# Decoder layer on one core: the rotary work of the next group of heads moved one step later on VectorE and GpSimd

## Chip, cores and metric

The kernel runs on 1 core of a Trainium2 chip. The metric is the device time of one launch in microseconds (us). Five engines work side by side, each through its own list of instructions in order: PE (TensorE: matmuls and their weight loads), ACT (ScalarE), DVE (VectorE), POOL (GpSimd) and SP (SyncE, which here only issues DMAs). They meet at semaphores alone.

## The reference, cut to what matters

Three stages follow each other: self-attention, a cross-attention with gathered neighbours, and a quantised feed-forward. The change touches only the first.

```python
# x: (4, 1024, 256), 16 heads of 64
q = (x @ wq.T + bq); k = (x @ wk.T + bk); v = (x @ wv.T + bv)      # per head
q, k = rope(q, k)              # x * cos + rotate(x) * sin, pairs of columns
scores = q k^T, causal; attn = softmax(scores / 8)
x = layernorm(x + (attn @ v) @ wo.T + bo)
...
```

## The kernel before

Self-attention is written as one list of instructions for each engine. Four heads make a group (16 groups, index `i`), two heads make a pair (32 pairs, index `n`, with `i, p = divmod(n, 2)`). A pair goes through six steps `m`. In each step PE computes two blocks ("units", `u = 2m, 2m+1`) of scores for pair `n`, multiplies the probabilities of the step before into the values (`weigh`), and then does the step's extra work (`step_uses`, line 86): chunks of scores of pair `n + 1`, from which the row maxima are taken, and one bigger item of `FULL_AT` (line 42).

The extra work of an even pair is the projection of q and k of the next group, in four parts, at steps 0, 2, 3 and 4 (below: part 0 to part 3); that of an odd pair is the output projection of the group before (steps 0 and 1) and the value projection (steps 2 and 4). Each part goes through three engines:

- ACT copies it from PSUM to SBUF (`stage`, line 602, the copy is line 608). There are two buffers `staged`, so `stage` of part `u` first waits until GpSimd has finished part `u - 2` (semaphore `s_rot`, line 607).
- DVE does four scalar_tensor_tensor instructions (`rotate`, line 699; lines 716 and 720), each of 128x512 float32: bias and multiplication with the cosine or sine table.
- GpSimd adds up the terms (`turn`, line 929; lines 935 and 936).

The row maxima take this way: PE makes a chunk (nine for a pair; in an even pair chunks 0 to 2 at step 1, 3 and 4 at step 2, 5 and 6 at step 3, 7 and 8 at step 4), ACT copies it negated in bfloat16 (line 570, three buffers), DVE masks it (line 767, chunks 0 to 4) and takes the minimum (lines 773 and 778). After chunk 8 DVE makes the negated maxima (`negate`, line 785), PE spreads them into a row in PSUM (`max_row`, line 440, matmul line 448), ACT copies the row (line 561), and PE adds it to the scores of the next pair (`shift`, line 477). `max_row` is the last thing PE does in a pair: until it is through, no score of the next pair is begun.

The probabilities: ACT takes the exponential of each unit (line 626), GpSimd zeroes the corner above the diagonal (`mask_probs`, line 898) and adds the unit to a running sum (`add_probs`, lines 916 and 919). Units 8 and 9 belong to step 4, units 10 and 11 to step 5. DVE also multiplies the output of the pair before by the inverse sums (`normalise`, line 798).

PSUM is handed out as a ring of three slots in PE's order of use (`slot_order`, `wait_slot`, line 244): each use waits until the third use before it has been read. At the end of an even pair the order is unit 8, unit 9, chunk 7, chunk 8, part 3 of the projection, unit 10, unit 11, row. So `max_row` waits for two things: for `negate` (line 442), and for ACT's copy of part 3 (line 257). ACT does that copy after the exponentials of units 8 and 9 and before those of units 10 and 11.

What sets the order around the change is the code itself: DVE's loop is lines 849 to 883, GpSimd's lines 950 to 963.

Of the kernel before, what the change touches and what calls it, by code (L numbers as in the profile page):

```python
# [38 lines left out]
QK_UNITS = 4  # L39
# [35 lines left out]
def full_at(n, m):  # L75

    i, p = divmod(n, 2)
    if not FULL_AT[p][m]:
        return None
    kind, u = FULL_AT[p][m]  # L80
    if kind == "out":
        return (kind, i - 1, u) if i else None
    return (kind, i + 1, u) if i + 1 < GROUPS else None


def step_uses(n, m):

    full = full_at(n, m)
    chunks = [("max", n + 1, c) for c in CHUNKS_AT[n % 2][m]] if n + 1 < PAIRS else []
    if m == 1:  # L90
        sums = [("den", n - 1, 0)] if n else []
        return ([full] if full else []) + chunks[:-1] + sums + chunks[-1:]
    if m == 2 and n % 2:
        return ([full] if full else []) + chunks
    return chunks + ([full] if full else [])
# [28 lines left out]
def attention(nc, dram, y, psum):  # L124

    ctx = ExitStack()
    with ctx:
# [568 lines left out]
        def _(dve):  # L696
            V = nc.vector

            def rotate(i, u):

                m = QK_UNITS * i + u
                hf, qk = divmod(u, 2)
                tok = slice(hf * BANK, (hf + 1) * BANK)
                ev, od = staged[m % 2][:, 0, :], staged[m % 2][:, 1, :]
                be, bo = (bqk[:, i % NG, 2 * qk + eo:2 * qk + eo + 1] for eo in range(2))
                tu = turned[:, :, qk, tok]
                dve.wait_ge(s_stage, m + 1)
                if u == 0 and i == 0:
                    dve.wait_ge(s_bqk, 16)
                if u == 0 and i:  # L710
                    for p in range(2):
                        dve.wait_ge(s_ops[p], 16 * STACK_DMAS * i)
                if i == 0:
                    dve.wait_ge(s_tab[hf], 16)
                for dst, x, b, table in ((tu[:, 0, :], ev, be, cosE), (tu[:, 1, :], od, bo, cosO)):
                    V.scalar_tensor_tensor(out=dst, in0=x, scalar=b, in1=table[:, tok], op0=ALU.add, op1=ALU.mult)\  # L716
                     .then_inc(s_term, 1)
                dve.wait_ge(s_term, TERMS * m + 2)
                for x, b, table in ((ev, be, sinO), (od, bo, sinE)):
                    V.scalar_tensor_tensor(out=x, in0=x, scalar=b, in1=table[:, tok], op0=ALU.add, op1=ALU.mult)\  # L720
                     .then_inc(s_term, 1)
# [127 lines left out]
            for n in range(PAIRS):  # L849
                i, p = divmod(n, 2)  # L850
                new_x = p == 1 and i % NG == 2 and i // NG + 1 < B
                for m in range(STEPS):
                    for kind, k, u in step_uses(n, m):
                        if kind == "max":
                            maximum(k, u)
                        elif kind == "out":
                            residual(k, u)
                    if m == 2 and n:
                        invert(n - 1)
                    if m == LAST_CHUNKS:  # L860
                        if n + 1 < PAIRS:
                            negate(n + 1)
                        if n:
                            normalise(n - 1)
                    if full_at(n, m) and full_at(n, m)[0] == "qk":
                        rotate(i + 1, full_at(n, m)[2])
                    if p == 1 and m == 0 and i + 1 < GROUPS:
                        low_v(i + 1)
                    if p == 1 and m == 1 and i + 2 < GROUPS:
                        for kt in range(KT):  # L870
                            low_qk(i + 2, kt)
                    if p == 1 and m < 2 and i >= NG and i % NG == 1:
                        row_statistics(i // NG - 1, m)
                    if p == 1 and m == 1 and i >= NG and i % NG >= 2:
                        normalise_rows(i // NG - 1, i % NG - 2)
                    if new_x and m == 3:
                        for piece in range(KT):
                            low_x(i // NG + 1, piece)
                    if p == 1 and m >= 4 and i % NG == 0:
                        add_bias(i // NG, m - 4)  # L880
                if new_x:
                    for piece in range(KT, X_PIECES):
                        low_x(i // NG + 1, piece)
# [6 lines left out]
        @block.gpsimd  # L890
        def _(pool):
            G = nc.gpsimd

            def mask_probs(n, u):

                pool.wait_ge(s_exp, NU * n + u + 1)
                block = probs[u % PBUF][:, :, 0:P]
                G.affine_select(block, block, [[0, 2], [1, P]], ALU.is_ge, 0.0, base=0, channel_multiplier=-1)\  # L898
                 .then_inc(s_tri, 1)

            def add_probs(n, u):

                k = NU * n + u
                kt, hf, a, width = span(u)
                if u in DIAGONAL:
                    pool.wait_ge(s_tri, len(DIAGONAL) * n + DIAGONAL.index(u) + 1)
                else:
                    pool.wait_ge(s_exp, k + 1)
                if u == 0 and n == 0:
                    pool.wait_ge(s_split, X_PIECES)  # L910
                if u == 0 and n >= 2:
                    pool.wait_ge(s_den, n - 1)
                dst = acc[n % 2][:, :, a:a + width]
                src = probs[u % PBUF][:, :, 0:width]
                if kt == 0:
                    G.tensor_copy(dst, src).then_inc(s_acc, 1)
                else:
                    pool.wait_ge(s_acc, k)
                    G.tensor_tensor(dst, dst, src, ALU.add).then_inc(s_acc, 1)  # L919

            def deviations(b):
                pool.wait_ge(s_avar, b + 1)
                if b:
                    pool.wait_ge(s_ax1, 2 * b)
                G.tensor_scalar(a_rstd[:, :], a_mv[:, :, 1], EPS, None, ALU.add).then_inc(s_adev, 1)
                pool.wait_ge(s_adev, b + 1)
                G.tensor_tensor(a_rstd[:, :], a_rstd[:, :], a_power[:, :], ALU.pow).then_inc(s_astd, 1)

            def turn(i, u):

                m = QK_UNITS * i + u
                hf, qk = divmod(u, 2)
                tu = turned[:, :, qk, hf * BANK:(hf + 1) * BANK]
                pool.wait_ge(s_term, TERMS * (m + 1))
                G.tensor_tensor(tu[:, 0, :], tu[:, 0, :], staged[m % 2][:, 1, :], ALU.subtract).then_inc(s_rot, 1)
                G.tensor_tensor(tu[:, 1, :], tu[:, 1, :], staged[m % 2][:, 0, :], ALU.add).then_inc(s_rot, 1)

            G.memset(a_power[:, :], -0.5).then_inc(s_set, 1)
            G.memset(ones[:, :], 1.0).then_inc(s_set, 1)
            G.memset(negz[:, :, :, :], 0.0).then_inc(s_set, 1)  # L940
            G.memset(first[:, :], 0.0).then_inc(s_set, 1)
            pool.wait_ge(s_set, 4)
            G.memset(first[0:1, :], 1.0).then_inc(s_set, 1)
            pool.wait_ge(s_set, 5)
            G.memset(first[D:D + 1, :], 1.0).then_inc(s_set, 1)
            pool.wait_ge(s_set, 6)
            G.memset(lows[:, :, :], 1e38).then_inc(s_set, 1)
            for u in range(QK_UNITS):
                turn(0, u)
            for n in range(PAIRS):  # L950
                i, p = divmod(n, 2)
                for m in range(STEPS):
                    for u in (2 * m, 2 * m + 1):
                        if u in DIAGONAL:
                            mask_probs(n, u)
                    if p == 1 and m == 0 and i + 1 < GROUPS:
                        turn(i + 1, QK_UNITS - 1)
                    for u in (2 * m, 2 * m + 1):
                        add_probs(n, u)
                    if p == 0 and m and full_at(n, m - 1) and full_at(n, m - 1)[2] < QK_UNITS - 1:  # L960
                        turn(i + 1, full_at(n, m - 1)[2])
                if i >= NG and i % NG == 1 and p == 1:
                    deviations(i // NG - 1)

# [1479 lines left out]
```

## Time and profile before

| | |
|---|---|
| median of three runs | 2231.85 us (2228.64 to 2235.41) |
| the profiled execution, its own time | 2232.63 us |
| its span, first to last instruction | 2230.7 us |
| busy PE, DVE, POOL, ACT over the span | 84%, 71%, 63%, 59% |
| self-attention | about 57 to 1375 us of the span |
| one group of self-attention (two pairs) | about 82 us |
| PE busy from 400 to 500 us | 94.06 of 100 us |
| PE idle before `max_row` (line 448), 60 to 1270 us | 35.2 us in 15 places |

The timeline views list an engine's instructions in order of time: start, duration (from the first start to the last end of a merged row), engine, line, operation, what is written and read, how many, and in brackets how long the engine was idle before it and what ended that. Two instructions of one engine may overlap in the record by a few hundredths of a microsecond. The duration of a DVE or POOL instruction includes time in which it has begun and is held up. Pairs repeat with small differences; the stretch around 509.55 us, the end of an even pair, is followed closely.

### The profile page before, as it was taken

To read this page: it belongs to the slowest core of one execution; us is meant where nothing else is said; L and a number is where in the kernel's file an instruction comes from. 1 tells how busy PE (TensorE), PEld (TensorE's weight loads), DVE (VectorE), ACT (ScalarE), POOL (GpSimd) and SP (SyncE) were. 2 spreads that over 40 slices of the span, in tenths; PEclk is the share of its full clock that TensorE was granted. 3 is DMA by queue.
4 is the path that set the end of the run, shared out by engine and by line. 5 is a ranking of instruction groups with operands and counts; after the bars stand their busy time and mean duration, and the time that the engine had idled before them with its cause. 6 is when DMAs were issued, how large, how long until landed. Compare 5 with 4: busy or idle time off the path is not lost. (4 is left out here: it accounts for less than half of the span.)

```text
span 2230.7 us, 42278 instructions
## 1 busy us (share of the span) xinstructions
PE 1864.7 (84%) x16907; PEld 1122.3 (50%) x16907; DVE 1593.3 (71%) x2216; ACT 1312.8 (59%) x1718; POOL 1410.0 (63%) x1067
## 2 busy tenths in 40 slices
PE   6899989999989999989999996588787787883675
PEld 3445545555545555545555543366565566663332
DVE  6775776776776776776776762668769768679676
ACT  3565565565565565565565561286856756873466
POOL 2877757777857877757877773344654555545347
PEclk8999999999999999999999998799988898997786
DMA  6122222222222222222222110100000000100002
GB/s 212 42 53 53 49 71 51 51 53 53 49 71 49 53 53 53 48 70 50 53 53 53 39 39 25 54 3 7 2 7 2 2 2 2 43 3 1 2 1 76
DMA packets 57507, 92.33 MB, mean 41 GB/s; under 512 B 25312, under 2 KB 35552, under 8 KB 53344
## 3 DMA queue, kind: packets, MB, share of 16 engines
q1 hardware_dynamic: 48096, 89.36, 16.0%
q8 instruction: 134, 2.20, 0.4%
q10 hardware_dynamic: 9216, 0.27, 0.2%
q14 instruction: 61, 0.50, 0.1%
HBM read 51.33 MB, written 4.46 MB: 25 GB/s over the span
## 5 line engine op out<-in xcount | busy, mean ns | idle before, releaser
L919 POOL TENSOR_TENSOR acc<-acc,probs 128x1024 f32<-128x1024 f32 (+3 forms) x320 | 592.2, 1851 | 149.9 <-ACT probs L626 121.1
L626 ACT ACTIVATE probs<-psum 128x1024 f32<-128x1024 f32 (+3 forms) x384 | 290.9, 812 | 139.7 <-PE psum L477 139.7
L570 ACT ACTIVATE chunks<-psum 128x1024 bf16<-128x1024 f32 x288 | 278.1, 1027 | 83.4 <-PE psum L436 60.4
L1478 ACT ACTIVATE onehot<-psum 128x1024 bf16<-128x1024 f32 x320 | 323.0, 1038 | 1.3 <-PE psum L1288 1.3
L469 PE MATMUL psum<-operands 64*128 64x512 f32 (+3 forms) x1536 | 308.4, 520 | 17.6 <-ACT chunks L570 17.2
L1885 POOL TENSOR_TENSOR vs<-vs,wgt 128x1280 f32<-128x1280 f32 x64 | 156.3, 2443 | 250.8 <-DVE wgt L1729 250.8
L1306 PE MATMUL psum<-pieces,onehot 128*128 128x64 bf16 x7680 | 289.4, 199 | 26.8 <-ACT vs L1485 19.5
L1306 PEld LDWEIGHTS psum<-pieces,onehot 128*128 128x128 bf16 x7680 | 261.0, 102 | 89.1 <-issue 45.3
L493 PE MATMUL psum<-probs,vals 128*64 128x512 f32 (+3 forms) x1536 | 292.6, 499 | 11.8 <-POOL probs L898 11.8
L773 DVE TENSOR_REDUCE lows<-chunks 128x2 f32<-128x1024 bf16 (+1 forms) x224 | 265.4, 1215 | 22.5 <-ACT chunks L570 11.4
L716 DVE SCALAR_TENSOR_TENSOR turned<-staged,bqk,rot 128x512 f32<-128x512 f32 x128 | 150.1, 1212 | 114.0 <-ACT staged L608 114.0
L898 POOL TENSOR_SCALAR_AFFINE_SELECT probs<-probs 128x256 f32<-128x256 f32 x256 | 144.5, 582 | 107.8 <-ACT probs L626 107.8
L767 DVE TENSOR_TENSOR chunks<-chunks,later 128x512 bf16<-128x512 bf16 (+1 forms) x160 | 122.8, 768 | 123.3 <-ACT chunks L570 123.3
L469 PEld LDWEIGHTS psum<-operands 64*128 64x128 f32 x1536 | 130.4, 189 | 148.3 <-issue 80.1
L1695 DVE TENSOR_TENSOR prod<-psum,xq 128x320 f32<-128x320 f32 x256 | 124.0, 488 | 109.4 <-PE psum L1306 104.5
L1485 ACT ACTIVATE vs<-psum 128x320 f32<-128x320 f32 x256 | 114.9, 449 | 147.2 <-DVE prod L1695 146.6
L1288 PE MATMUL psum<-i0T,near 32*128 32x512 bf16 x640 | 131.5, 411 | 82.4 <-ACT onehot L1478 76.0
L720 DVE SCALAR_TENSOR_TENSOR staged<-staged,bqk,rot 128x512 f32<-128x512 f32 x128 | 183.9, 1475 | 2.3
L493 PEld LDWEIGHTS psum<-probs,vals 128*64 128x64 f32 x1536 | 93.1, 136 | 159.0 <-issue 143.5
L436 PE MATMUL psum<-operands 64*128 64x512 f32 (+3 forms) x768 | 118.5, 397 | 38.7 <-ACT probs L626 18.7
L420 PE MATMUL psum<-wo,ctxT 128*128 128x256 f32 x512 | 120.5, 389 | 11.4 <-DVE ctxT L798 11.4
L436 PEld LDWEIGHTS psum<-operands 64*128 64x128 f32 x768 | 58.7, 188 | 131.2 <-issue 59.8
(228 smaller groups left out, 3331.2 us busy)
## 6 DMA issues: line engine op xcount, KB each, us to landing
operands<-turned SPq DMA_DIRECT2D x124, 256.0 KB, 4.2
rden<-inverse_rows SPq DMA_DIRECT2D x64, 256.0 KB, 4.0
raw<-in_wqk SPq DMA_DIRECT2D x30, 256.0 KB, 4.5
y<-in_x SPq DMA_DIRECT2D x1, 4096.0 KB, 16.3
wo<-in_wo SPq DMA_DIRECT2D x16, 256.0 KB, 3.2
out<-res SPq DMA_DIRECT2D x16, 256.0 KB, 2.1
raw<-in_wv SPq DMA_DIRECT2D x15, 256.0 KB, 4.4
raw<-in_xT SPq DMA_DIRECT2D x12, 256.0 KB, 4.4
```

Source lines behind the costliest of these rows:

```text
L436: last = nc.tensor.matmul(dst[:, hh, col:col + width], ops[p][rows, 0, qt * P:(qt + 1) * P], ops[p][rows, 1, hf * BANK:hf * BANK + width], ...
L469: nc.tensor.matmul(dst[:, hh, 0:width], ops[n % 2][rows, 1, kt * P:(kt + 1) * P].bitcast(F32), ops[n % 2][rows, 0, a:a + width].bitcast(F3 ...
L493: last = nc.tensor.matmul(obank[rows, hf, a - hf * BANK:BANK], vals[i % 2][:, kt, 2 * p + hh, :], probs[u % PBUF][:, hh, 0:width], start=k ...
L570: nc.scalar.activation(chunks[k % MBUF][:, :, :], slot("max", n, c)[:, :, :], ACT.Copy, scale=-1.0)\
L626: nc.scalar.activation(probs[u % PBUF][:, :, 0:width], slot("s", n, u)[:, :, 0:width], ACT.Exp, scale=1.0 / D ** 0.5).then_inc(s_exp, 1)
L716: V.scalar_tensor_tensor(out=dst, in0=x, scalar=b, in1=table[:, tok], op0=ALU.add, op1=ALU.mult)\
L720: V.scalar_tensor_tensor(out=x, in0=x, scalar=b, in1=table[:, tok], op0=ALU.add, op1=ALU.mult)\
L773: V.tensor_reduce(lows[:, :, place_of[0]:place_of[-1] + 1:step], src[:, :, 0:len(parts) * width].rearrange("p h (k q) -> p h k q", q=width ...
L919: G.tensor_tensor(dst, dst, src, ALU.add).then_inc(s_acc, 1)
L1306: last = nc.tensor.matmul(out, onehot[:, n % 2, k, tok:tok + P], pieces[b % 2][p][:, h, :, :].rearrange("p (s c) d -> p s (c d)", s=2), st ...
L1478: A.activation(onehot[:, n % 2, k, :], bc[m % 2], ACT.Relu).then_inc(s_oh, 1)
L1885: G.tensor_tensor(v, v, w.broadcast_to([P, TT * NK * 2, HD]), ALU.mult).then_inc(s_wm, 1)
```

## The change

In an even pair DVE's rotation of a part now comes one step later. Part 0, projected at step 0, is rotated at step 1 behind chunks 0 to 2; part 1 at step 3 behind chunks 5 and 6; part 2 at step 4 behind chunks 7 and 8, `negate` and `normalise`; part 3 at step 5. GpSimd's `turn` of parts 0, 1 and 2 also comes one step later: at the ends of steps 2, 4 and 5 instead of 1, 3 and 4. `turn` of part 3 stays at step 0 of the odd pair. PE, ACT and SP keep their order word for word, and no instruction is added or removed. The last group has nothing to project, so 15 even pairs are touched.

```diff
@@ DVE, the loop over steps
-                    if full_at(n, m) and full_at(n, m)[0] == "qk":
-                        rotate(i + 1, full_at(n, m)[2])
+                    if p == 0 and m and full_at(n, m - 1):
+                        rotate(i + 1, full_at(n, m - 1)[2])
@@ GpSimd, the loop over steps
-                    if p == 0 and m and full_at(n, m - 1) and full_at(n, m - 1)[2] < QK_UNITS - 1:
-                        turn(i + 1, full_at(n, m - 1)[2])
+                    if p == 0 and m > 1 and full_at(n, m - 2) and full_at(n, m - 2)[2] < QK_UNITS - 1:
+                        turn(i + 1, full_at(n, m - 2)[2])
```

DVE, even pair, from the reciprocal in step 2 to the first residual of the odd pair, before:

```order
L790 RECIPROCAL rcol<-dcol 128x16
L716 SCALAR_TENSOR_TENSOR turned<-staged1,bqk,rot 128x512 x2
L720 SCALAR_TENSOR_TENSOR staged1<-staged1,bqk,rot 128x512 x2
L773 TENSOR_REDUCE lows<-chunks2 128x2
L773 TENSOR_REDUCE lows<-chunks0 128x2
L716 SCALAR_TENSOR_TENSOR turned<-staged0,bqk,rot 128x512 x2
L720 SCALAR_TENSOR_TENSOR staged0<-staged0,bqk,rot 128x512 x2
L773 TENSOR_REDUCE lows<-chunks1 128x2
L773 TENSOR_REDUCE lows<-chunks2 128x2
L785 TENSOR_TENSOR negmax<-lows 128x16
L798 TENSOR_TENSOR ctxT<-osum1,rden 128x1024
L716 SCALAR_TENSOR_TENSOR turned<-staged1,bqk,rot 128x512 x2
```

The same stretch of DVE after:

```order
L790 RECIPROCAL rcol<-dcol 128x16
L773 TENSOR_REDUCE lows<-chunks2 128x2
L773 TENSOR_REDUCE lows<-chunks0 128x2
L716 SCALAR_TENSOR_TENSOR turned<-staged1,bqk,rot 128x512 x2
L720 SCALAR_TENSOR_TENSOR staged1<-staged1,bqk,rot 128x512 x2
L773 TENSOR_REDUCE lows<-chunks1 128x2
L773 TENSOR_REDUCE lows<-chunks2 128x2
L785 TENSOR_TENSOR negmax<-lows 128x16
L798 TENSOR_TENSOR ctxT<-osum1,rden 128x1024
L716 SCALAR_TENSOR_TENSOR turned<-staged0,bqk,rot 128x512 x2
L720 SCALAR_TENSOR_TENSOR staged0<-staged0,bqk,rot 128x512 x2
L716 SCALAR_TENSOR_TENSOR turned<-staged1,bqk,rot 128x512 x2
```

Between the reciprocal and `negate` (L785) stood two rotations; now one stands there, that of part 1, behind chunks 5 and 6, and the rotation of part 2 stands behind `normalise`.

GpSimd, even pair, steps 3 to 5, before (the first row is the sum of unit 7):

```order
L919 TENSOR_TENSOR acc0<-acc0,probs3 128x2x512
L935 TENSOR_TENSOR turned<-turned,staged1 128x512
L936 TENSOR_TENSOR turned<-turned,staged1 128x512
L898 AFFINE_SELECT probs0<-probs0 128x2x128
L898 AFFINE_SELECT probs1<-probs1 128x2x128
L919 TENSOR_TENSOR acc0<-acc0,probs0 128x2x512
L919 TENSOR_TENSOR acc0<-acc0,probs1 128x2x384
L935 TENSOR_TENSOR turned<-turned,staged0 128x512
L936 TENSOR_TENSOR turned<-turned,staged0 128x512
L898 AFFINE_SELECT probs2<-probs2 128x2x128
```

The same stretch of GpSimd after:

```order
L919 TENSOR_TENSOR acc0<-acc0,probs3 128x2x512
L898 AFFINE_SELECT probs0<-probs0 128x2x128
L898 AFFINE_SELECT probs1<-probs1 128x2x128
L919 TENSOR_TENSOR acc0<-acc0,probs0 128x2x512
L919 TENSOR_TENSOR acc0<-acc0,probs1 128x2x384
L935 TENSOR_TENSOR turned<-turned,staged1 128x512
L936 TENSOR_TENSOR turned<-turned,staged1 128x512
L898 AFFINE_SELECT probs2<-probs2 128x2x128
L898 AFFINE_SELECT probs3<-probs3 128x2x128
L919 TENSOR_TENSOR acc0<-acc0,probs2 128x2x256
```

The end of part 1 (`staged1`) stood ahead of the masks and sums of units 8 and 9; it now stands behind them.

## Rows read from the trace of the kernel before

**Rows 1.** The waits of PE, 60 to 1270 us: total, times, longest.

```profile
PE psum L448 <- DVE negmax L785: 35.2, 15, 3.3
```

**Rows 2.** All engines, 504 to 514 us: the rows of PE around `max_row`.

```profile
505.55 1.72 PE L493 MATMUL psum<-probs,vals 128*64 128x512 f32 x8
...
509.55 0.64 PE L448 MATMUL psum<-ident,negmax 128*64 128x128 bf16 x16 [2.28 <-DVE negmax L785]
...
512.66 0.65 PE L493 MATMUL psum<-probs,vals 128*64 128x256 f32 x4 [0.39 <-POOL probs L898]
...
513.47 0.44 PE L493 MATMUL psum<-probs,vals 128*64 128x128 f32 x4 [0.16 <-POOL probs L898]
...
513.84 0.48 PE L420 MATMUL psum<-wo,ctxT 128*128 128x256 f32 x1
```

**Rows 3.** Timeline of DVE, 498 to 512 us.

```profile
502.95 3.56 DVE L720 SCALAR_TENSOR_TENSOR staged<-staged,bqk,rot 128x512 f32<-128x512 f32 x2
506.44 2.33 DVE L773 TENSOR_REDUCE lows<-chunks 128x2 f32<-128x1024 bf16 x2
508.81 0.69 DVE L785 TENSOR_TENSOR negmax<-lows 128x16 bf16<-128x16 f32 x1
509.36 1.21 DVE L798 TENSOR_TENSOR ctxT<-osum,rden 128x1024 f32<-128x1024 f32 x1
```

**Rows 4.** Timeline of ACT, 494 to 513 us.

```profile
498.99 1.73 ACT L626 ACTIVATE probs<-psum 128x1024 f32<-128x1024 f32 x2 [0.41 <-PE psum L477]
501.45 1.94 ACT L570 ACTIVATE chunks<-psum 128x1024 bf16<-128x1024 f32 x2 [0.74 <-PE psum L436]
504.64 1.03 ACT L608 ACTIVATE staged<-psum 128x1024 f32<-128x1024 f32 x1 [1.25 <-PE psum L383]
505.60 0.87 ACT L626 ACTIVATE probs<-psum 128x512 f32<-128x512 f32 x2
```

**Rows 5.** Timeline of POOL, 491 to 514 us.

```profile
503.16 5.03 POOL L919 TENSOR_TENSOR acc<-acc,probs 128x1024 f32<-128x1024 f32 x2
508.15 1.25 POOL L935 TENSOR_TENSOR turned<-turned,staged 128x512 f32<-128x512 f32 x1
509.37 2.33 POOL L936 TENSOR_TENSOR turned<-turned,staged 128x512 f32<-128x512 f32 x1
```

**Rows 6.** Rotary instructions, 100 to 1250 us: min/median/max ns, first and last start.

```profile
L716 DVE SCALAR_TENSOR_TENSOR turned<-staged,bqk,rot x108: 659/887/2884, 139.6 to 1243.7; 128x512 f32<-128x512 f32 x108
L720 DVE SCALAR_TENSOR_TENSOR staged<-staged,bqk,rot x109: 739/1747/2869, 98.6 to 1249.3; 128x512 f32<-128x512 f32 x109
L936 POOL TENSOR_TENSOR turned<-turned,staged x54: 1260/1280/2332, 103.0 to 1233.8; 128x512 f32<-128x512 f32 x54
```

**Rows 7.** Timeline of POOL in an odd pair: mask and sums of units 8, 9.

```profile
461.92 0.41 POOL L898 TENSOR_SCALAR_AFFINE_SELECT probs<-probs 128x256 f32<-128x256 f32 x1 [0.29 <-ACT probs L626]
462.29 2.37 POOL L919 TENSOR_TENSOR acc<-acc,probs 128x1024 f32<-128x1024 f32 x1
...
464.80 1.85 POOL L919 TENSOR_TENSOR acc<-acc,probs 128x768 f32<-128x768 f32 x1
```

**Rows 8.** Timelines of ACT and POOL at step 2 of the even pair.

```profile
483.27 1.02 ACT L570 ACTIVATE chunks<-psum 128x1024 bf16<-128x1024 f32 x1 [1.26 <-DVE lows L778]
...
486.45 2.39 POOL L919 TENSOR_TENSOR acc<-acc,probs 128x1024 f32<-128x1024 f32 x1
```

**Rows 9.** Timeline of PE at another end of an even pair.

```profile
426.80 1.06 PE L448 MATMUL psum<-ident,negmax 128*64 128x128 bf16 x16 [2.27 <-DVE negmax L785]
...
431.87 0.92 PE L420 MATMUL psum<-wo,ctxT 128*128 128x256 f32 x3
```

**Rows 10.** Stretches of 2 us from `max_row` on: length, busy of each engine, PE clock.

```profile
95.38:97.38 2.00, 2.00 (x20) 1.32 (x22) 2.00 (x2) 1.02 (x1) 2.00 (x3) 0.59 0.00 0
...
426.80:428.80 2.00, 2.00 (x18) 1.32 (x20) 2.00 (x2) 0.90 (x1) 2.00 (x1) 0.51 0.02 4
509.55:511.55 2.00, 2.00 (x24) 1.26 (x26) 2.00 (x2) 1.02 (x1) 2.00 (x1) 1.00 0.00 0
```

## The prediction

> **What bounds the kernel now.** I read the busy shares first: PE is busy for 94 of the 100 us from 400 to 500 in self-attention, so a change there pays only where it shortens a place at which PE itself stands still. The second view is PE's waits. The largest is that of `max_row` for DVE's negated maxima: 35.2 us in 15 places, one at the end of each even pair from the first to the 15th [rows 1]. That is 1.6% of the time, and it is what this change can reach. The third view is the timeline around one of them. PE has finished its last weighting at 507.27 (505.55 + 1.72) and starts `max_row` at 509.55, after 2.28 us of nothing [rows 2]. On DVE the second half of part 2's rotation runs until 506.51, then the maxima of chunks 7 and 8 until 508.77, then `negate` until 509.50 [rows 3]. Those chunks lay copied since 503.39 (501.45 + 1.94) [rows 4]. So DVE's rotation of part 2 is in the way, and the change moves it behind.
>
> **Two waits, not one.** `max_row` also waits, through the ring of PSUM slots, for ACT's copy of part 3, and that copy waits for GpSimd's end of part 1, since both use the same staging buffer. Before, the copy ran at 504.64 to 505.67, as soon as PE had projected the part [rows 4], long before `max_row`, so this second wait does not show. The change moves GpSimd's end of part 1 from ahead of the sums of units 8 and 9 to behind them. The question is when it is through then.
>
> **Walk of the changed order, in the stretch that ends at 509.55.** PE, ACT and SP keep their order and their times up to the first new wait. Four durations carry it: a rotation instruction takes 0.66 or 0.74 us undisturbed (minima, against maxima of 2.88 and 2.87), `turn`'s second 1.26 us undisturbed against 2.33 at worst [rows 6], the sums of units 8 and 9 2.37 and 1.85 us and a mask 0.41 beside DVE work that reads one tensor [rows 7]. The large values arise where DVE and GpSimd both want to run an instruction on two SBUF tensors: the one that comes second does not progress until the first is through. The clearest row: GpSimd's second `turn` instruction, 509.37 with 2.33 us, lies over `normalise`, 509.36 to 510.57, and ends 1.13 us behind it [rows 3, 5].
>
> 1. Chunk 2 is copied at 484.29 (483.27 + 1.02) [rows 8]. Mask and minimum take about 1.7 us, so rotation 0 starts at 486.0. One of its instructions runs before GpSimd's sum of unit 5 (2.39 us) [rows 8], three behind it: 486.9, 489.3, then 3 x 0.7: done at 491.4.
> 2. GpSimd's end of part 0 (2 x 1.26) alternates with the masks of chunks 3 and 4 on DVE (estimated at 0.3 each): done at 494.7. ACT needs it for part 2's copy at 497: 2.4 us to spare, price nothing. Chunks 3 and 4 are read by 495.9 (the masks and two minima of 1.2 to 1.3 us each; the nearest row is 2.33 for two minima [rows 3]). Their buffers are wanted again at 494.8 (chunk 3, read at 493.2) and at 501.45: free.
> 3. Sums 6 and 7 on GpSimd, 2 x 2.37 from 494.7: 499.4. Minima of chunks 5 and 6 on DVE: 498.3. Rotation 1 waits for sum 7, then alternates with the masks of units 8 and 9, whose exponentials end by 500.72 (498.99 + 1.73) [rows 4]: 499.4 + 2 x 0.66 + 2 x 0.74 gives 502.2; the masks fall in between.
> 4. Minima of chunks 7 and 8 from 502.5, held by the copy that ends at 503.39: done 504.8. Sums 8 and 9 on GpSimd from 502.2: 504.6, then 506.5. `negate` needs two tensors and waits for that: 506.5, which is 0.8 before PE wants it. **The wait that the change aims at is gone**: -2.28 us at this place, if nothing else were late.
> 5. GpSimd's end of part 1: behind `normalise` (1.1, as between 509.50 and 510.57 [rows 3]) and 2 x 1.26: 506.5 + 1.1 + 2.5 = 510.1. ACT's copy of part 3: 510.15 + 1.03 [rows 4] = 511.2. `max_row` starts at 511.25 instead of 509.55: **+1.7 us**, and PE stands still for 4.0 us instead of 2.28. ACT's exponentials of units 10 and 11 stand behind that copy; they end at 512.1 (0.87 [rows 4]) and PE's next scores need them only from about 511.9 and 512.8 on.
> 6. What comes back at once: before, PE waited another 0.39 and 0.16 us for the masks of units 10 and 11 [rows 2]. Now these come ahead of GpSimd's end of part 2, right behind the exponentials, so I count the 0.55 as gone: from `max_row` to the output projection 4.29 us becomes 3.74. That end moves from 513.84 to 514.99: **+1.15 us**.
>
> Rotations 2 and 3 then run on DVE from about 508 to 517; the residual that follows them waits for an output projection that ends near 518.5, so they cost nothing. GpSimd's end of part 3 slips by about 2 us; its operands are wanted some 10 us later. If either cover fails it would show as a new wait in the odd pair; I put no price on it. Nothing in the odd pair gives the loss back: PE is busy throughout.
>
> **The clock.** After the idle time PE sometimes runs at the lower level. At 426.80 the granted clock is 0.51 (1.2 GHz), and 5.07 us pass until the output projection; at 509.55 it is 1.00 (2.4 GHz) and 4.29 pass [rows 2, 9, 10]. Of the 15 places 5 show this, 10 don't, the one with 3.3 us of idle time among the 5 [rows 1, 10]. An idle time of 4.0 us has no row. Bounds: the same 5, or all 15. I take 10, half-way, since the longest idle time fell and two thirds of the 2.3 us ones didn't. The Trainium skill says on this (TensorE: Matmul & The Clock Gate, Part 1) that "the default state is throttled, and activity releases the throttle". By that rule the longer standstill would put more places at the low level, nearer to all 15, which is the upper bound below.
>
> **The sum.** A place at full clock before and after costs 1.15; one that was low before and stays low costs 1.7 (5.07 on both sides); one that becomes low costs 511.25 + 5.07 - 513.84 = 2.5. With 5 of each: 5 x 1.15 + 5 x 1.7 + 5 x 2.5 = 26.7 us. On the profiled execution's own 2232.63 that is 2259.4; the median shown lies 0.8 below that execution, so I say **2259**, 1.2% slower.
>
> **Rivals.**
>
> *Faster, about 2216.* DVE and GpSimd meet less often than I let them. Without any holding-up the masks are through at 501.2, the sums at 505.5, the end of part 1 at 508.0, ACT's copy at 509.1: `max_row` starts 0.45 early and the output projection is reached 1.0 early: 15 x 1.0 = 15 us less; with a shorter idle time up to 5 x 0.8 more: 2213 to 2218. For it: the masks of chunks and the negation are short. Against it: an L720 takes 1.75 us in the median against 0.74 alone [rows 6], so meeting is the rule here. The point from which it decides: the end of part 1 before about 508.5. The Trainium skill (SBUF — State Buffer, the reading of its port diagram) calls the pair of ports shared by the two engines an exclusive lock that is held for the whole instruction. By that rule the two-tensor work of both engines adds up from 486 on, which is the walk above, 2259; if the two only slowed each other in part, it would be this rival. The 2.33 us row agrees with the rule.
>
> *No change, 2226 to 2238.* One holding-up less than in the walk, for example if the end of part 1 gets ahead of `normalise` and rotation 1 is out of GpSimd's way earlier: the end at 508.9 to 509.2, `max_row` at about 510.1: +0.55 - 0.55 = 0 at the output projection, and a few us for the clock either way.
>
> *Slower still, 2266 to 2275.* All 15 places at the low level: 5 x 1.7 + 10 x 2.5 = 33.5, that is 2266. If a rotation instruction also gets between the two of `turn`, 0.6 more at 15 places: 2275.
>
> *The change does not do what it says.* The negation could still be last, if rotation 1 ran beyond 505; then the maxima of chunks 7 and 8 end after 507.3. That needs 3 us more than in step 3 and would come together with a still later end of part 1, so its time is that of the case above.
>
> **How the numbers follow.** Forecast (2239 to 2265) 0.60; slower still 0.12; no change 0.14; faster 0.14. A measurement of this kernel can tell about 0.3%, 6.7 us, from no change. So faster 0.14, same 0.14, slower 0.72. For the range I leave out the faster rival and the outermost few per cent above 2272: 2228 to 2272, which holds the lower half of "no change" and the bounds of the clock.
>
> **What would show it.** Right: PE's wait at `max_row` is put down to ACT's copy of part 3 (L608), not to L785, 15 times at about 4 us; that copy is ended by GpSimd's L936; L785 ends before PE's last weighting; the waits for L898 behind it shrink; more stretches with a clock near 0.5. Wrong in step 5: the copy starts by 508. Wrong in the cover: a new wait in the odd pairs, for the operands or the residual.

## The result and the profile after

The changed kernel takes 2278.17 us (median of four runs, 2273.97 to 2280.74) against 2233.27 us for the kernel before (four runs): a ratio of 1.0209, 95% interval 1.0186 to 1.0233. It is slower by 45 us. The forecast was 2259 us, slower by 27, with a range up to 2272. So the sign and the wait were right, and the time lies outside the range.

The waits of PE in self-attention, 60 to 1320 us of the changed kernel (total, times, longest; it answers [rows 1]):

```profile
PE psum L448 <- ACT staged L608: 60.3, 15, 4.1
PE psum L436 <- ACT probs L626: 17.0, 17, 4.2
```

`max_row` still waits at 15 places, now for ACT's copy of part 3, and for 60.3 us instead of 35.2: 3.04 us at the first place and 4.07 to 4.11 at the other 14. The timeline of PE around one of the places (it answers [rows 2]):

```profile
520.28 1.72 PE L493 MATMUL psum<-probs,vals 128*64 128x512 f32 x8
526.08 1.06 PE L448 MATMUL psum<-ident,negmax 128*64 128x128 bf16 x16 [4.07 <-ACT staged L608]
527.07 3.36 PE L469 MATMUL psum<-operands 64*128 64x512 f32 x8
530.22 0.96 PE L477 MATMUL psum<-bias,first_rows 64*128 64x512 bf16 x4
531.11 0.94 PE L493 MATMUL psum<-probs,vals 128*64 128x256 f32 x8
531.98 0.70 PE L420 MATMUL psum<-wo,ctxT 128*128 128x256 f32 x2
```

PE is through at 522.00 and idle for 4.07 us; then 5.90 us pass until the output projection, where it was 4.29. The other three engines over the same stretch, DVE first (it answers [rows 3]):

```profile
512.29 2.38 DVE L716 SCALAR_TENSOR_TENSOR turned<-staged,bqk,rot 128x512 f32<-128x512 f32 x2
514.71 1.56 DVE L720 SCALAR_TENSOR_TENSOR staged<-staged,bqk,rot 128x512 f32<-128x512 f32 x2
517.31 2.35 DVE L773 TENSOR_REDUCE lows<-chunks 128x2 f32<-128x1024 bf16 x2 [1.04 <-ACT chunks L570]
519.69 1.26 DVE L785 TENSOR_TENSOR negmax<-lows 128x16 bf16<-128x16 f32 x1
520.82 1.21 DVE L798 TENSOR_TENSOR ctxT<-osum,rden 128x1024 f32<-128x1024 f32 x1
521.95 3.41 DVE L716 SCALAR_TENSOR_TENSOR turned<-staged,bqk,rot 128x512 f32<-128x512 f32 x2
```

POOL (it answers [rows 5]):

```profile
516.51 4.36 POOL L919 TENSOR_TENSOR acc<-acc,probs 128x1024 f32<-128x1024 f32 x2
520.82 2.33 POOL L935 TENSOR_TENSOR turned<-turned,staged 128x512 f32<-128x512 f32 x1
523.11 1.70 POOL L936 TENSOR_TENSOR turned<-turned,staged 128x512 f32<-128x512 f32 x1
```

ACT (it answers [rows 4]):

```profile
524.91 1.02 ACT L608 ACTIVATE staged<-psum 128x1024 f32<-128x1024 f32 x1 [6.79 <-POOL turned L936]
525.83 0.87 ACT L626 ACTIVATE probs<-psum 128x512 f32<-128x512 f32 x2
```

The negation is ready at 520.95, 1.05 us before PE wants it: the wait that the change aims at is gone. GpSimd begins the end of part 1 only behind both sums, at 520.82; `normalise` and one rotation instruction get in between, it is done at 524.81, ACT's copy at 525.93, `max_row` starts at 526.08.

The clock, in stretches of 2 us from `max_row` on, and for the 5.90 us (it answers [rows 10]; the third column from the right is PE's granted clock):

```profile
97.00:99.00 2.00, 2.00 (x20) 1.14 (x22) 2.00 (x4) 1.64 (x3) 1.58 (x3) 0.70 0.00 0
...
526.08:528.08 2.00, 2.00 (x18) 1.32 (x20) 2.00 (x4) 1.52 (x3) 1.59 (x3) 0.50 0.00 0
...
526.08:531.98 5.90, 5.90 (x36) 2.87 (x36) 5.12 (x6) 2.73 (x5) 5.34 (x5) 0.56 0.00 0
```

The first place reads 0.70 and each of the other 14 reads 0.50, the level of 1.2 GHz. Before, 5 of 15 were below 1.00.

**Where the 45 us are.** The spans differ by 44.7 us (2275.4 against 2230.7). PE's waits at `max_row` grew by 60.3 - 35.2 = 25.1 us. From `max_row` to the output projection the timeline gives 5.9 to 6.2 us at each of 14 places (the first place has no such projection), 5.98 in the mean, where it gave 4.29 ten times and 5.1 four times, 4.52 in the mean: 14 x 1.46 = 20.4 us. Together 45.5. Two smaller differences nearly cancel and are not in this sum. Up to `max_row` of the 16th even pair, which begins at 1379.75 and began at 1330.98, the kernel is 48.8 us longer, about 3 more than these two, and they lie in the first group. From there to the end it takes 895.7 us instead of 899.7; the code there is the same, and the 12 traces of this case give 889 to 909 us for it, so a few microseconds between two single traces say nothing.

### The profile page after: what moved, and what is told of

Its sections match the earlier page's. It is cut to its first block and busy times, and to the rows that moved or that the text cites. A ratio compares the mean times of both kernels' runs of the same rounds, so it can differ in the third digit from the quotient of the medians.

```text
span 2275.4 us, 42278 instructions
## 1 busy us (share of the span) xinstructions
PE 1886.7 (83%) x16907; PEld 1129.5 (50%) x16907; DVE 1526.6 (67%) x2216; ACT 1310.6 (58%) x1718; POOL 1386.5 (61%) x1067
## 5 line engine op out<-in xcount | busy, mean ns | idle before, releaser
L919 POOL TENSOR_TENSOR acc<-acc,probs 128x1024 f32<-128x1024 f32 (+3 forms) x320 | 573.5, 1792 | 97.2 <-ACT probs L626 68.7
L626 ACT ACTIVATE probs<-psum 128x1024 f32<-128x1024 f32 (+3 forms) x384 | 290.8, 812 | 157.3 <-PE psum L477 155.0
L469 PE MATMUL psum<-operands 64*128 64x512 f32 (+3 forms) x1536 | 325.5, 544 | 17.6 <-ACT chunks L570 17.2
L773 DVE TENSOR_REDUCE lows<-chunks 128x2 f32<-128x1024 bf16 (+1 forms) x224 | 264.8, 1213 | 37.1 <-ACT chunks L570 26.3
L767 DVE TENSOR_TENSOR chunks<-chunks,later 128x512 bf16<-128x512 bf16 (+1 forms) x160 | 93.8, 586 | 289.7 <-ACT chunks L570 289.7
L898 POOL TENSOR_SCALAR_AFFINE_SELECT probs<-probs 128x256 f32<-128x256 f32 x256 | 132.5, 535 | 152.9 <-ACT probs L626 152.9
L469 PEld LDWEIGHTS psum<-operands 64*128 64x128 f32 x1536 | 135.4, 196 | 154.8 <-issue 87.5
L716 DVE SCALAR_TENSOR_TENSOR turned<-staged,bqk,rot 128x512 f32<-128x512 f32 x128 | 175.6, 1410 | 15.5 <-ACT staged L608 15.5
L608 ACT ACTIVATE staged<-psum 128x1024 f32<-128x1024 f32 x64 | 65.7, 1026 | 185.1 <-POOL turned L936 108.0
L916 POOL COPY acc<-probs 128x1024 f32<-128x1024 f32 x64 | 66.5, 1040 | 149.0 <-ACT probs L626 149.0
L436 PE MATMUL psum<-operands 64*128 64x512 f32 (+3 forms) x768 | 119.0, 399 | 37.5 <-ACT probs L626 17.3
L935 POOL TENSOR_TENSOR turned<-turned,staged 128x512 f32<-128x512 f32 x64 | 105.9, 1655 | 51.7 <-DVE staged L720 51.7
```

The lines of the kernel that those rows point to most:

```text
L469: nc.tensor.matmul(dst[:, hh, 0:width], ops[n % 2][rows, 1, kt * P:(kt + 1) * P].bitcast(F32), ops[n % 2][rows, 0, a:a + width].bitcast(F3 ...
L626: nc.scalar.activation(probs[u % PBUF][:, :, 0:width], slot("s", n, u)[:, :, 0:width], ACT.Exp, scale=1.0 / D ** 0.5).then_inc(s_exp, 1)
L773: V.tensor_reduce(lows[:, :, place_of[0]:place_of[-1] + 1:step], src[:, :, 0:len(parts) * width].rearrange("p h (k q) -> p h k q", q=width ...
```

## The experiments

All times below stand beside runs of the kernel before on the same chip, 2232 to 2233 us in the median. The changed kernel was timed once, beside 2233.27 us, so a difference from it may be off by a microsecond or two. Timelines are those of one profiled execution each, which is not always near the median of its kernel (e6_part2_only: 2196.83 against 2206.56 us).

**One half of the change alone.** First the rotations on VectorE, with GpSimd's order as before.

```diff
# against the kernel before
-                    if full_at(n, m) and full_at(n, m)[0] == "qk":
-                        rotate(i + 1, full_at(n, m)[2])
+                    if p == 0 and m and full_at(n, m - 1):
+                        rotate(i + 1, full_at(n, m - 1)[2])
```

> VectorE's rotations stand as in the changed kernel, GpSimd's ends of parts 0 to 2 stand as in the kernel before (part 1 ahead of the masks and sums of units 8 and 9). Theory (the late end of part 1 on GpSimd is what costs): ScalarE's copy of part 3 is no longer late by much, max_row's wait of 4.1 us for it is gone or under 1 us; what is left is that GpSimd stands waiting for rotations with masks behind it, about +-0.5 us a place, so 2225 to 2245 us. Rival (the later rotations on VectorE are what costs, wherever GpSimd's ends stand): as slow as the changed kernel, 2265 to 2280 us.

Measured: 2326.87 us, ratio 1.0432 (1.0407 to 1.0458). Neither expectation. No wait for L448 is left, as the theory said, but PE's timeline shows another one behind it:

```profile
445.93 0.65 PE L448 MATMUL psum<-ident,negmax 128*64 128x128 bf16 x16
...
455.71 1.55 PE L493 MATMUL psum<-probs,vals 128*64 128x256 f32 x8 [7.06 <-POOL probs L898]
```

and POOL's timeline tells why:

```profile
451.38 1.71 POOL L935 TENSOR_TENSOR turned<-turned,staged 128x512 f32<-128x512 f32 x1 [1.29 <-DVE staged L720]
453.05 1.70 POOL L936 TENSOR_TENSOR turned<-turned,staged 128x512 f32<-128x512 f32 x1
454.71 1.67 POOL L898 TENSOR_SCALAR_AFFINE_SELECT probs<-probs 128x256 f32<-128x256 f32 x2
```

GpSimd stands waiting for rotation 2, then ends part 2, and the masks of units 10 and 11 are queued behind that; PE waits 7 us for them. I had priced this at 0.5 us. So GpSimd's end of part 2 had to be moved with its rotation; the change is right in that.

**The other half**, GpSimd's ends one step later and the rotations as before:

```diff
# against the kernel before
-                    if p == 0 and m and full_at(n, m - 1) and full_at(n, m - 1)[2] < QK_UNITS - 1:
-                        turn(i + 1, full_at(n, m - 1)[2])
+                    if p == 0 and m > 1 and full_at(n, m - 2) and full_at(n, m - 2)[2] < QK_UNITS - 1:
+                        turn(i + 1, full_at(n, m - 2)[2])
```

> GpSimd's ends stand as in the changed kernel, VectorE's rotations as in the kernel before. Theory: the end of part 1 stands behind the sums of units 8 and 9 all the same, so max_row waits for ScalarE's copy of part 3 at 15 places, some 3 to 4 us each, and the clock falls at most of them: 2262 to 2280 us. Rival (VectorE's order is what costs): max_row waits for the negated maxima as before, 2228 to 2240 us.

Measured: 2296.03 us, ratio 1.0293 (1.0266 to 1.032), 16 us above the upper end that I expected. `max_row` waits 5.67 us at each of 15 places, and the profile names DVE's negation, not ACT's copy. DVE's timeline:

```profile
523.06 4.50 DVE L716 SCALAR_TENSOR_TENSOR turned<-staged,bqk,rot 128x512 f32<-128x512 f32 x2
527.60 3.31 DVE L720 SCALAR_TENSOR_TENSOR staged<-staged,bqk,rot 128x512 f32<-128x512 f32 x2
...
533.20 0.92 DVE L785 TENSOR_TENSOR negmax<-lows 128x16 bf16<-128x16 f32 x1
```

and PE's:

```profile
534.18 1.07 PE L448 MATMUL psum<-ident,negmax 128*64 128x128 bf16 x16 [5.67 <-DVE negmax L785]
```

Rotation 2 now runs beside the two sums and the end of part 1 on GpSimd, one instruction of each in turn: its four instructions take 7.85 us, where undisturbed they take 2.8 [rows 6]. ACT's copy of part 3 is late as the theory had it (81.6 us of waits for L936 in 14 places): it ends at 531.48, 2.97 us behind PE's last weighting (528.51), and the negation, done at 534.12, is later still. GpSimd's half alone is therefore enough for a loss, by both ways at once; with both halves together the negation is out of it. The granted clock is 0.50 behind each of the 15 waits of 5.67 us.

**Only the end of part 1 put back ahead of the sums**, everything else as changed:

```diff
# against the changed kernel, GpSimd
                     for u in (2 * m, 2 * m + 1):
                         if u in DIAGONAL:
                             mask_probs(n, u)
...
+                    if p == 0 and m == 4 and full_at(n, 2):
+                        turn(i + 1, 1)
                     for u in (2 * m, 2 * m + 1):
                         add_probs(n, u)
-                    if p == 0 and m > 1 and full_at(n, m - 2) and full_at(n, m - 2)[2] < QK_UNITS - 1:
+                    if p == 0 and m in (2, 5) and full_at(n, m - 2) and full_at(n, m - 2)[2] < QK_UNITS - 1:
                         turn(i + 1, full_at(n, m - 2)[2])
```

> The changed kernel with one instruction pair of GpSimd put elsewhere: the end of part 1 stands ahead of the sums of units 8 and 9, behind their masks. Theory: ScalarE's copy of part 3 comes by about 505 in the frame of the prediction, the negated maxima by 507, and both waits of max_row are gone: 2.28 us less than before at 15 places and the clock stays up, 2192 to 2203 us. Rival (the loss comes from several places and GpSimd being behind everywhere): the time stays above 2240 us.

Measured: 2229.94 us, ratio 0.9991 (0.9977 to 1.0005). Moving this pair of instructions takes 48 us off the changed kernel, which settles what the loss hung on; but the gain of 30 us and more that I expected is not there. PE's timeline:

```profile
507.31 0.62 PE L448 MATMUL psum<-ident,negmax 128*64 128x128 bf16 x16
...
510.69 0.65 PE L493 MATMUL psum<-probs,vals 128*64 128x256 f32 x4 [0.67 <-POOL probs L898]
...
518.42 3.18 PE L493 MATMUL psum<-probs,vals 128*64 128x512 f32 x8 [1.81 <-ACT probs L626]
```

`max_row` starts with no wait. Waits for the masks of units 10 and 11 (0.67 and 0.16 us) are back, and a larger one stands at step 1 of the odd pair, 25.4 us in 14 places. It is put down to L626, the exponentials, but those ended at 511.6; the masks of units 0 and 1 are what came last, as POOL shows:

```profile
514.12 1.71 POOL L935 TENSOR_TENSOR turned<-turned,staged 128x512 f32<-128x512 f32 x1
515.79 1.71 POOL L936 TENSOR_TENSOR turned<-turned,staged 128x512 f32<-128x512 f32 x1
517.46 1.67 POOL L898 TENSOR_SCALAR_AFFINE_SELECT probs<-probs 128x256 f32<-128x256 f32 x2
```

The end of part 2 stands ahead of those masks. At this place PE then runs at the lower level for a while: the eight matmuls take 3.18 us, and over the 3.2 us from 518.4 on the granted clock is 0.52. But only one other of the 14 places is like this; at the other 12, behind the same 1.81 us, the clock over the next 2 us is 1.00 (at 436.75 the eight matmuls take 1.72 us). The gain went to waits: 35.2 us for the negation and 7.1 for masks (L898) before, now 25.4 and 12.3, and 5.5 at step 1 of the first odd pair.

**The standstill filled.** This takes the clock alone. TensorE does 17 more matmuls in the wait; their output is overwritten and nothing depends on it.

```diff
# against the changed kernel, TensorE, ahead of max_row
+                if p == 0 and i + 1 < GROUPS:
+                    pe.wait_ge(s_oc, 2 * n + 1)
+                    for _ in range(17):
+                        nc.tensor.matmul(obank[:, 0, :], ident[:, :], bias[n % 2][:, 0:BANK], start=True, stop=True)
                 if n + 1 < PAIRS:
                     max_row(n + 1)
```

> The changed kernel, and TensorE does 17 further matmuls of 128x512 bfloat16 (about 3.7 us at 2.4 GHz) between its last weighting and max_row at the 15 places, into a half of the output bank that is free then; their result is overwritten and not used. Theory (half of the loss is the clock that falls after the standstill): max_row starts where it did, the granted clock there is 1.00 instead of 0.50, the 5.9 us from max_row to the output projection become 3.7 to 4.3, so 14 x 1.6 to 2.2 = 22 to 31 us less than the changed kernel: 2247 to 2256 us. Rival (the clock does not depend on the standstill, or the slow stretch is slow for another reason): 2275 to 2282 us, or more if the matmuls outlast the wait.

Measured: 2243.49 us, ratio 1.0047 (1.0031 to 1.0064). That is 34.7 us less than the changed kernel, more than expected. PE's timeline (of the fastest of ten executions, 2234.8 us; four added lines make the copy of part 3 L612 and the filling L548):

```profile
512.08 3.84 PE L548 MATMUL psum<-bias,ident 128*128 128x512 bf16 x17
516.25 0.64 PE L448 MATMUL psum<-ident,negmax 128*64 128x128 bf16 x16 [0.33 <-ACT staged L612]
516.82 1.77 PE L469 MATMUL psum<-operands 64*128 64x512 f32 x8
...
519.70 0.70 PE L420 MATMUL psum<-wo,ctxT 128*128 128x256 f32 x2
```

`max_row` waits for the same copy to the same moment, 4.1 us behind the last weighting (512.14), and the granted clock is 1.00 at all 15 places. Now 3.45 us pass until the output projection, at each of 14 places. So 5.98 - 3.45 = 2.53 us a place is the price of the standstill beyond its own length, 14 x 2.53 = 35 us, which is what the medians say (34.7).

**`normalise` out of the way of the end of part 1.**

```diff
# against the changed kernel, VectorE
-                        if n:
+                        if n and (p or i + 1 == GROUPS):
                             normalise(n - 1)
+                    if m == STEPS - 1 and n and p == 0 and i + 1 < GROUPS:
+                        normalise(n - 1)
```

> The changed kernel with normalise of an even pair moved from step 4 to step 5, behind the rotation of part 2. Theory (step 5 of the prediction: GpSimd's end of part 1 is also held up by normalise, 1.1 us): TensorE stands still before max_row for about 3.0 us instead of 4.08; the clock still falls at most of the places, so 15 x 1.1 = 16 us less, 2258 to 2266 us. Rival (something else takes normalise's turn, since a rotation instruction is next in line): the idle time stays at 3.6 to 4.1 us and the time at 2270 to 2280 us.

Measured: 2256.89 us, ratio 1.01 (1.0069 to 1.013). PE's timeline and three stretches of 2 us from `max_row` on (the profiled execution is the fastest of four, 2247.77 us):

```profile
516.87 0.64 PE L448 MATMUL psum<-ident,negmax 128*64 128x128 bf16 x16 [3.03 <-ACT staged L608]
```

```profile
516.87:518.87 2.00, 2.00 (x20) 1.22 (x22) 2.00 (x3) 1.64 (x3) 1.58 (x2) 0.68 0.00 0
600.46:602.46 2.00, 2.00 (x18) 1.32 (x20) 2.00 (x3) 1.52 (x3) 1.58 (x2) 0.50 0.03 8
775.16:777.16 2.00, 2.00 (x24) 1.26 (x26) 2.00 (x3) 1.64 (x3) 1.58 (x2) 1.00 0.00 0
```

The standstill is 1.05 us shorter, the 1.1 of step 5. The median falls by 21 us and not by 15 because the clock gives something back too. At 5 of the 15 places it now stays at 1.00 and 3.45 us pass until the output projection; at 7 of the 9 low places that have one, 4.9 to 5.1 us pass, and at 2 still 6.2. In the trace that is 14.8 us less in waits at `max_row`, 18.6 less in these stretches and 6.5 more in a new wait, 1.3 us at step 1 of the odd pair at each of the 5 fast places. Together 26.9; up to `max_row` of the 16th even pair the trace is 26.7 us shorter.

**The same filling in the kernel before**, 9 matmuls in its 2.28 us.

> The kernel before, with 9 further matmuls of 128x512 bfloat16 (1.9 us) in TensorE's wait of 2.28 us at the 15 places. Theory: the clock no longer falls at the 5 places where it did, 0.8 us each, so 3 to 6 us less than before: 2226 to 2230 us. Rival (the falls come from the load as a whole and not from the standstill): no change, 2230 to 2235 us, with clocks of 0.5 at about 5 places still.

Measured: 2231.45 us, ratio 0.9993 (0.9979 to 1.0008). The clock reads 1.00 at all 15 places and each of the 14 stretches takes 4.29 us, so the falls do come from the standstill. In the time it can't be told from no change: the 3 to 6 us expected are within the noise.

**Towards a kernel that keeps the gain.** Only the rotation of part 2 goes behind the negation; parts 0, 1 and 3 stay as before, and GpSimd ends part 2 behind the masks of units 0 and 1 of the odd pair.

```diff
# against the kernel before
-                    if full_at(n, m) and full_at(n, m)[0] == "qk":
+                    if full_at(n, m) and full_at(n, m)[0] == "qk" and full_at(n, m)[2] != 2:
+                        if m == 4:
+                            rotate(i + 1, 2)
                         rotate(i + 1, full_at(n, m)[2])
...
                     if p == 1 and m == 0 and i + 1 < GROUPS:
+                        turn(i + 1, QK_UNITS - 2)
                         turn(i + 1, QK_UNITS - 1)
...
-                    if p == 0 and m and full_at(n, m - 1) and full_at(n, m - 1)[2] < QK_UNITS - 1:
+                    if p == 0 and m in (1, 3) and full_at(n, m - 1) and full_at(n, m - 1)[2] < QK_UNITS - 1:
                         turn(i + 1, full_at(n, m - 1)[2])
```

> Against the kernel before: VectorE's rotation of part 2 alone goes behind negate and normalise, GpSimd's end of part 2 goes behind the masks of units 0 and 1 of the odd pair; parts 0, 1 and 3 stay as before. Theory (the negation was worth moving something behind it, only part 1's end on GpSimd and the masks must not be late): no wait at max_row, none or little for the masks of units 10, 11, 0 and 1, the clock at 1.00 at all 15 places: 2.3 to 3.1 us less at each, 2183 to 2200 us. Rival (a gap only turns up elsewhere, as in the run where part 1's end was put early): 2222 to 2236 us.

Measured: 2206.56 us, ratio 0.9884 (0.9841 to 0.9927), 7 us above the interval of the theory and well below that of the rival. No wait is left at `max_row`, and the clock there is 1.00 at all 15 places. The largest wait of PE is a new one, for the residual:

```profile
PE psum L420 <- DVE y L808: 20.6, 14, 1.6
```

The changed kernel's rotations with the same two placings on GpSimd:

> The changed kernel with GpSimd's end of part 1 ahead of the sums of units 8 and 9, as in e3_turn1_early, and its end of part 2 behind the masks of units 0 and 1 of the odd pair instead of ahead of them. Theory (e3_turn1_early gave its gain back at step 1 of the odd pair, where TensorE waits 1.8 us for the masks of units 0 and 1 and then runs at the lower clock): that wait goes, 3 to 3.8 us less at each of 15 places than e3_turn1_early: 2175 to 2200 us. Rival (GpSimd has too much to do there in any order): 2220 to 2235 us.

Measured: 2221.19 us, ratio 0.9945 (0.9925 to 0.9965): better than e3_turn1_early by 9 us, not by the 45 to 57 of the expectation, and inside the rival's interval. The wait of 1.81 us is gone at 14 places, as the theory said, but I had priced the lower clock at all of them, and it was at 2. Unlike e3_turn1_early, which shows no such wait, it waits for the residual (13.1 us in 14 places), and the 0.64 and 0.16 us for the masks of units 10 and 11 remain, since the end of part 1 stands ahead of the sums and these ahead of the masks.

Then `normalise` of an even pair is moved to step 3, into a gap of DVE ahead of the copy of chunk 7:

```diff
# against e6_part2_only, VectorE
-                        if n:
+                        if n and p:
                             normalise(n - 1)
+                    if m == 3 and n and p == 0:
+                        normalise(n - 1)
```

> e6_part2_only with normalise of an even pair moved from behind the negation to step 3, ahead of chunks 7 and 8, where VectorE stands waiting for a copy of 0.8 to 1.3 us. Theory (what is left in e6_part2_only is VectorE being 1.5 us late with the residual in the odd pair, because rotations 2 and 3 and normalise all stand behind the negation): the wait of TensorE for line 808 falls from 1.46 us to under 0.5 us at 14 places, 12 to 18 us less, 2188 to 2196 us. Rival (normalise waits at step 3 for the inverse sums, which land about then, and makes the negation late): TensorE waits for line 785 again, 2205 to 2235 us.

Measured: 2192.99 us, ratio **0.9817** (0.9792 to 0.9843), inside the expected interval. At the first 15 even pairs no wait for L448 or L420 is left, nor one for a mask between `max_row` and the output projection, as PE's timeline shows, and the clock there is 1.00:

```profile
493.54 0.62 PE L448 MATMUL psum<-ident,negmax 128*64 128x128 bf16 x16
494.09 1.77 PE L469 MATMUL psum<-operands 64*128 64x512 f32 x8
495.70 0.55 PE L477 MATMUL psum<-bias,first_rows 64*128 64x512 bf16 x4
496.17 0.87 PE L493 MATMUL psum<-probs,vals 128*64 128x256 f32 x8
496.97 3.72 PE L420 MATMUL psum<-wo,ctxT 128*128 128x256 f32 x16
```

The 16th even pair, which projects nothing, pays for it:

```profile
1287.65 1.06 PE L448 MATMUL psum<-ident,negmax 128*64 128x128 bf16 x16 [6.31 <-DVE negmax L785]
```

`normalise` was moved there too. It waits 5.08 us for the DMA of the inverse sums (`rden`) and holds up the maxima of chunks 7 and 8 behind it, and the clock falls to 0.50: the rival's mechanism, at one place. In the kernel before this wait was 0.85 us and 3.45 us passed until the output projection, now 5.14. Against e6_part2_only 20.6 us of waits for the residual are gone and about 7 (5.5 + 1.7) have come, which agrees with the 13.6 us between the medians. Leaving `normalise` of that pair where it was should give back those 7 us, an estimate from these rows; no run has it.

Last, in this kernel the end of part 2 goes back to step 5:

> e9_norm_early with GpSimd's end of part 2 back at step 5 of the even pair, ahead of the masks of units 0 and 1 of the odd pair (as in the changed kernel). Theory (masks behind both ends make TensorE wait at step 1 of the odd pair, which alone took the gain of e3_turn1_early): a wait of about 1 to 2 us for line 898 or 626 shows again at 15 places and the clock falls at some of them, 20 to 40 us more than e9_norm_early. Rival (e3_turn1_early lost its gain through part 1's end ahead of the sums, not through part 2's end): within 8 us of e9_norm_early.

Measured: 2212.55 us, ratio 0.9901 (0.9869 to 0.9933), 19.6 us more than without it, just under the 20 to 40 expected. PE waits 1.42 us at step 1 of the odd pair, 19.7 us in 14 places:

```profile
507.54 1.73 PE L493 MATMUL psum<-probs,vals 128*64 128x512 f32 x8 [1.42 <-ACT probs L626]
```

The named exponentials had ended at 502.25; the two masks ran from 506.58 to 507.80. The clock stays at 1.00 behind all 14, so the falls that I expected did not come. That place is thus a second cost in the change's order. In the changed kernel it doesn't show, since PE is late there already: the 14 waits are absent.

## Why the prediction was wrong, point by point

**Steps 1 to 4 of the walk** held to within 1 us. The negation is ready 1.05 us before PE wants it; forecast was 0.8.

**Step 5** held in its result: `max_row` waits for ACT's copy of part 3, ended by GpSimd's L936, at 15 places, 4.07 to 4.11 us at 14 of them where 4.0 was forecast (3.04 at the first). The total of 60.3 us is 25.1 more than before; the sum had 15 x 1.7 = 25.5. Inside the step, one rotation instruction more got in between and the sums began a little earlier; the two errors cancel. e5_norm_late measures `normalise`'s part at 1.05 us against 1.1.

**Step 6** held in kind: the waits for the masks of units 10 and 11 are gone. At full clock (e4_fill) 3.45 us pass where I had 3.74. The cover for the later rotations and ends held as well, but with PE late: e3_turn1_early and e10_turn2_ahead show that the end of part 2 makes PE wait in the odd pair once PE is on time.

**The clock is the step that failed.** It had two sizes, both too small. I took 10 of 15 places at the lower level, half-way between bounds; it was 15. And I took 5.07 us from `max_row` to the output projection for a low place, from a row that stands behind a standstill of 2.27 us; behind one of 4.07 us it is 5.98 in the mean, since the low level lasts through the scores and the shift (3.36 and 0.96 us for L469 and L477, against 1.77 and 0.54 at full clock, and 2.97 and 0.54 at the place of my row, where the clock was back within the scores). By my terms this stretch was to add 1.2 us in the sum: 5 x 0.78 newly low, less 5 x 0.55 for the masks. It added 20.4. The difference of 19 us is all of the distance from 2259 to 2278. e4_fill shows that it is the standstill: with the same wait filled, the time falls by 34.7 us.

The Trainium skill's rule (TensorE: Matmul & The Clock Gate, Part 1), by which activity releases the throttle, pointed at the upper bound. I had cited it and still gone half-way. The trace agrees with it at all 15 places.

**The range.** Its upper end had all 15 places low at the price of one at 2.3 us of idle time, 2266, and a little more. With 5.98 for the price the same case gives 2280. The bound of the number was in the range, the bound of the price was not.

**The rivals.** "Slower still", 2266 to 2275 with a chance of 0.12, came nearest. Its all-low case came true; the rotation instruction got between the two of `turn`, too, but the sums began early enough to pay for it, so its 0.6 us a place didn't show. Like the forecast it priced a low place too low. "Faster" and "no change" needed DVE and GpSimd to meet less often; the rows show them taking turns as in the walk. "The change does not do what it says" fell too.

## What to carry to other kernels

When work is moved behind a wait, list every semaphore that the waiting instruction needs, those of slots and buffers too, and follow each back through the engines: here the aimed-at wait went, and a copy two engines away took its place. A standstill of TensorE costs its length and the clock behind it, and here both the chance and the price of the lower clock grew with the length; price the clock for the new length, not from rows at the old one. What is moved should be the one item in the way: a single rotation behind the negation, with its counterpart behind the masks and `normalise` in a gap, gave 1.8%, while moving all of them lost 2.1%.

## What the runs showed of the hardware

- How often the granted clock fell below 1.00 in the 2 us behind an idle time of PE, at places that repeat once a group: 1.4 us none of 14 (e10_turn2_ahead; 1.4 to 1.6 us none of 14 in e6_part2_only), 1.81 us 2 of 14 (e3_turn1_early), 2.24 to 2.29 us 4 of 14 (kernel before, which was also low behind 3.3 us at its first place), 3.03 us 10 of 15 (e5_norm_late), 4.07 to 4.11 us 14 of 14 (changed kernel, which was also low behind 3.04 us at its first place), 5.67 us 15 of 15 (e2_pool_only). With the wait filled by matmuls none of 15, in both kernels.
- The price grows too. The stretch from `max_row` to the output projection takes 3.45 us at full clock without a wait for masks. At low places it took 5.1 us behind 2.3 us of idle time, 4.9 to 6.2 behind 3.0, and 5.9 to 6.2 behind 4.1. In the kernel before a place at full clock took 4.29, with waits for masks that a low place doesn't have, so a fall cost only 0.8 there.
- A very short VectorE instruction on two SBUF tensors is held up for as long as GpSimd's: the negation took 0.23 us undisturbed in an odd pair of the kernel before (467.14), 1.26 us in the changed one and 1.80 in e3_turn1_early (505.17). When both engines had such work queued they took turns instruction by instruction, and four rotation instructions took 7.85 us in place of 2.8 (e2_pool_only). A minimum over one tensor was not held up: the 193 of L773 between 100 and 1250 us of the kernel before all took 1.20 to 1.22 us. That agrees with the Trainium skill (SBUF — State Buffer, the reading of its port diagram), which calls the shared pair an exclusive lock.
